# A DLRM tower on one core: the lookup of the last two tables goes behind the third lookup of the second step, and the Gram products of the first two tiles one lookup further down

## Chip, cores and metric

The kernel runs on one core of one Trainium2 chip. The metric is the device time of one execution in microseconds (us); the lower, the better. Engines are named as in the profile: PE (TensorE, matmuls), DVE (VectorE), ACT (ScalarE), POOL (GpSimd), SP (SyncE, which here only issues DMAs).

## What is computed

For each of 2048 items, 26 embedding rows of 128 numbers are looked up, set beside the item's dense vector, and all pairs of the 27 vectors are multiplied. The 351 products and the dense vector go through three layers.

```python
e = jnp.stack([tbl_f[ids[:, f]] for f in range(26)], axis=1)
combined = jnp.concatenate([e, r_dense_x[:, None, :]], axis=1)
z = jnp.einsum('bfd,bgd->bfg', combined, combined)[:, triu_i, triu_j]
h = jnp.concatenate([z.reshape(B, -1), r_dense_x], axis=1)
h = jnp.maximum(h @ W_top1 + b_top1, 0.0)      # 479 -> 512
h = jnp.maximum(h @ W_top2 + b_top2, 0.0)      # 512 -> 256
y = h @ W_top3                                 # 256 -> 1
```

## The kernel before

The 2048 items are cut into 16 tiles of 128; two tiles are a step, so there are 8 steps, counted from 0, and step 0 holds tiles 0 and 1. Each engine runs a program written out by hand, in order, and waits on semaphores.

The ten tables of 1000 rows are not gathered but multiplied by one-hot matrices on PE. Two such tables are a **unit**: `unit(t, o)` looks up tables 2o and 2o+1 for step t with 32 matmuls, in 8 fills of 4. Each fill needs one one-hot matrix, made by DVE (L620, six of the eight in steps 0 to 2) or ACT (L426 and L432, the other two); there are 12 one-hot buffers. `keep_unit` on ACT (L438) copies a unit's result out of PSUM. A table must first be loaded into `stage` and split into a high part (ACT, `chunk`, L417) and a low part (DVE, `chunk`, L610). The tables come in one after the other, table pair 4 (chunks 8 and 9) last. In the first two steps the units of both steps are mixed so that few tables are needed early; `FIRST_ORDER` sets that order, and with it the numbering of the one-hot fills on all engines.

The other 16 tables are gathered by POOL, one indirect DMA for each table and tile (L285, 256 in all). Four tables of one tile are a **quad**; the rows go through a ring of 8 buffers, and `quad(tile, k)` on PE (L768) transposes them.

`products(tile)` on PE (L783) makes the **Gram** products of one tile, in four banks of 16 matmul pairs that alternate between two PSUM buffers. It needs all five units of the tile's step. DVE (L638) copies banks 0 and 2, and ACT (L453) banks 1 and 3, into the one buffer `gram`. From the second tile on these copies first wait until the tile before has left `gram`. SP sends `gram` to DRAM (`spread`, 8 DMAs, L333, landing counted by `turn_out`) and fetches it back in another layout (`fetch_z`, 7 DMAs, L342). Layer 1 of step 0 on PE (L807, L809) stands behind the fourth quad of tile 2 and waits for `z` of both tiles 0 and 1:

```python
                if bank == 0:
                    for u in range(2):
                        pe.wait_ge(z_in[u], Z_DMAS * 16 * (t + 1))
```

SP's queue is in order as well. `load_ids(t, o)` (L311) brings the ids from which the one-hots of a unit are made; it waits until the ids that lay in that place have been used. Between the fetch of tile 0 and the spread of tile 1, SP issues the three loads of the layers' weights (`load_weights`, L321 to L323) and two loads of ids.

Of the kernel before, what the change touches and what calls it, by code (L numbers as in the profile page):

```python
# [29 lines left out]
FILLS = KT  # L30
BUFS = 12
ACT_STEPS, ACT_FILLS = 3, 2
DVE_FILLS = FILLS - ACT_FILLS
# [12 lines left out]
PIECES = ((0, OH_P // 16 * 16), (OH_P // 16 * 16, OH_P))  # L46
RING = 8

FIRST_ORDER = ((0, 0), (1, 0), (0, 1), (0, 2), (1, 1), (0, 3), (0, 4), (1, 2), (1, 3), (1, 4))

FIRST_PLACES = (2, 3, 4, 5, 0, 1, 2, 3, 4, 5)

# [46 lines left out]
def tower_kernel(nc, x, ids_g, ids_oh, gathered, oh_tables, w1_pairs, w1_dense, w2, w3, b1, b2, out):  # L99
    ctx = ExitStack()  # L100
    with ctx:
# [106 lines left out]
        def last_made(t):  # L208

            return (DVE_FILLS if t < ACT_STEPS else FILLS) - 1  # L210
# [87 lines left out]
        def _(sp):  # L298
# [5 lines left out]
            def load_ids(t, o):  # L304
                before = ids_before(t, o)
                if before:
                    sp.wait_ge(onehot_made, made_by_dve(*before, last_made(before[0])))
                    if act_makes(before[0], FILLS - 1):
                        sp.wait_ge(onehot_act, made_by_act(*before, FILLS - 1))
                i = ids_at(t, o)  # L310
                sp.dma_start(ids_b[:, i], ids_oh[t, o].partition_broadcast(P)).then_inc(ids_in[i], 16)  # L311
# [13 lines left out]
            def spread(tile):  # L325
                u = tile % 2
                for h in range(2):
                    sp.wait_ge(gram_kept[h], GBANKS // 2 * (tile + 1))
                if tile >= 2:
                    sp.wait_ge(z_in[u], Z_DMAS * 16 * (tile // 2))  # L330
                for s in range(S4 // 2 if tile == TILES - 1 else S4):
                    for src, to in strip_out(u, s):
                        sp.dma_start(to, src).then_inc(turn_out[u], 16)  # L333
# [41 lines left out]
                sp.dma_start(dst[:], src).then_inc(small_in, 16)  # L375
            load_x(1)
            load_ids(2, 0)
            spread(0)

            load_ids(2, 1)  # L380
            load_ids(2, 2)
            sp.wait_ge(chunk_l, NOH)
            fetch_z(0)
            load_weights()
# [28 lines left out]
        def _(act):  # L413
# [20 lines left out]
            def keep_unit(t, o):  # L434
                n = unit_at(t, o)
                act.wait_ge(onehot_used, fill_at(t, o, FILLS - 1) + 1)
                a = NV + UNIT * o
                nc.scalar.copy(by_vector(t % 2, a, a + UNIT, 0, STEP), ps_o[n % 2][:].rearrange("p f b -> p b f")).then_inc(unit_kept, 1)  # L438
# [9 lines left out]
            def keep_gram(tile):  # L448
                if tile:
                    act.wait_ge(turn_out[(tile - 1) % 2], TURN_DMAS * 16 * ((tile + 1) // 2))  # L450
                for h in range(1, GBANKS, 2):
                    act.wait_ge(gram_done, GBANKS * tile + h + 1)
                    nc.scalar.copy(gram_of(h), products_of(h)).then_inc(gram_kept[h % 2], 1)  # L453
# [68 lines left out]
            keep_unit(1, 1)  # L522
            keep_quad(1, 0)
            chunk(8)
            make(0, 4)
            keep_unit(0, 3)
            keep_quad(1, 1)
            chunk(9)
            make(1, 2)
            keep_unit(0, 4)  # L530
            keep_quad(1, 2)
            make(1, 3)
            keep_unit(1, 2)
            keep_gram(0)
            keep_quad(1, 3)
            make(1, 4)
            keep_unit(1, 3)
            keep_gram(1)
            make(2, 0)
            keep_unit(1, 4)  # L540
            act.wait_ge(small_in, 48)
            for t in range(1, STEPS - 1):
                a, b = 2 * t, 2 * t + 1
# [61 lines left out]
        @block.vector  # L605
        def _(dve):
            def chunk(n):
                dve.wait_ge(chunk_h, n + 1)
                at, (hi, lo) = parts_of(n)
                nc.vector.tensor_tensor(lo, at, f32(hi), ALU.subtract).then_inc(chunk_l, 1)  # L610

            def make(t, o, h):
                n = fill_at(t, o, h)
                if act_makes(t, h):
                    return
                if h == 0:
                    dve.wait_ge(ids_in[ids_at(t, o)], ids_loaded(t, o))
                if n >= BUFS:
                    dve.wait_ge(onehot_used, n - BUFS + 1)
                nc.vector.tensor_scalar(onehot[n % BUFS][0:OH_P, 0:FILL].rearrange("p (a b) -> p a b", a=RUNS),  # L620
                                        ids_b[0:OH_P, ids_at(t, o), :, 0:RUN], row_of[0:OH_P, h:h + 1], None, ALU.is_equal
                                        ).then_inc(onehot_made, 1)

            def makes(t, first, end):
                if t < STEPS:
                    for n in range(first, end):
                        make(t, n // FILLS, n % FILLS)

            def makes_of(n, first, end):

                t, o = FIRST_ORDER[n]
                makes(t, FILLS * o + first, FILLS * o + end)

            def keep_bank(tile, h):
                if tile and h == 0:
                    dve.wait_ge(turn_out[(tile - 1) % 2], TURN_DMAS * 16 * ((tile + 1) // 2))
                dve.wait_ge(gram_done, GBANKS * tile + h + 1)
                nc.vector.tensor_copy(gram_of(h), products_of(h)).then_inc(gram_kept[h % 2], 1)  # L638

            def keep_gram(tile):  # L640
                for h in range(0, GBANKS, 2):
                    keep_bank(tile, h)

            def keep_y(t):
                dve.wait_ge(w3_done, t + 1)
                if t:
                    dve.wait_ge(y_out, 32 * t)
                for u in range(2):
                    last = by_item(u)
                last.then_inc(y_made, 1)  # L650

            def by_item(u):
                p = HALF_P * u
                return nc.vector.tensor_copy(y_sb[p:p + 1, :].rearrange("p (g s) -> p s g", s=S4),  # L654
                                             ps_l[1][p:p + 1, 0, 0:TILE].rearrange("p (s g) -> p s g", s=S4))

            def keep_tail(u):
                dve.wait_ge(w3_done, STEPS + u)
                if u == 0:
                    dve.wait_ge(y_out, 32 * (STEPS - 1))  # L660
                by_item(u).then_inc(y_made, 1)

            dve.wait_ge(consts_made, 2)
            nc.vector.tensor_copy(row_of[:], row_i[:]).then_inc(row_made, 1)
            for i in range(2):
                nc.vector.memset(ps_g[i][:], 0.0).then_inc(gram_zeroed, 1)
            dve.wait_ge(row_made, 1)
            ALL = UNITS * FILLS
            makes_of(0, 0, DVE_FILLS)
            chunk(0)  # L670
            makes_of(1, 0, 2)
            chunk(1)
            makes_of(1, 2, 4)
            chunk(2)
            makes_of(1, 4, DVE_FILLS)
            chunk(3)
            makes_of(2, 0, DVE_FILLS)
            chunk(4)
            makes_of(3, 0, 3)
            chunk(5)  # L680
            makes_of(3, 3, DVE_FILLS)
            makes_of(4, 0, DVE_FILLS)
            chunk(6)
            makes_of(5, 0, 3)
            chunk(7)
            makes_of(5, 3, DVE_FILLS)
            chunk(8)
            makes_of(6, 0, 3)
            chunk(9)
            makes_of(6, 3, DVE_FILLS)  # L690
            makes_of(7, 0, DVE_FILLS)
            makes_of(8, 0, 2)
            keep_bank(0, 0)
            makes_of(8, 2, 4)
            keep_bank(0, 2)
            makes_of(8, 4, DVE_FILLS)
            makes_of(9, 0, 4)
            keep_bank(1, 0)
            makes_of(9, 4, DVE_FILLS)
            keep_bank(1, 2)  # L700
            makes(2, 0, BUFS)
            for t in range(1, STEPS - 1):
                a, b = 2 * t, 2 * t + 1
                makes(t + 1, BUFS, 4 * FILLS)
                keep_gram(a)
                makes(t + 1, 4 * FILLS, ALL)
                makes(t + 2, 0, FILLS)
                if t < STEPS - 2:
                    keep_y(t - 1)
                    keep_gram(b)  # L710
                    makes(t + 2, FILLS, BUFS)
                else:
                    keep_gram(b)
                    keep_y(t - 1)
            t, a, b = STEPS - 1, TILES - 2, TILES - 1
            keep_gram(a)
            keep_gram(b)
            keep_y(t - 1)
            keep_tail(0)
            keep_tail(1)  # L720

        @block.tensor
        def _(pe):
# [173 lines left out]
            quad(1, 0)  # L897
            unit(0, 3)
            quad(1, 1)
            unit(0, 4)  # L900
            quad(1, 2)
            unit(1, 2)
            products(0)
            quad(1, 3)
            unit(1, 3)
            products(1)
            unit(1, 4)
            pe.wait_ge(small_in, 48)
            for t in range(1, STEPS - 1):
                a, b = 2 * t, 2 * t + 1  # L910
# [101 lines left out]
```

## Time and profile before

| | us |
|---|---|
| median of 3 runs | 361.75 (360.04 to 362.33) |
| the profiled execution, its own time | 362.72 |
| its span, first to last instruction | 360.9 |
| PE busy | 335.2 (93%) |
| POOL busy | 247.5 (69%) |
| DVE busy | 229.0 (63%) |
| ACT busy | 155.2 (43%) |

The profile is one execution. Starts are in microseconds from the span's start. A timeline row merges like instructions that follow each other; the brackets at its end give the idle time before it and what ended that. The granted clock is a share of 2.4 GHz: 1.00 is 2.4 GHz, 0.50 is 1.2 GHz.

### The profile page before, as it was taken

The numbers are of one execution on the slowest core, as the hardware profiler recorded it, in microseconds if no ns is written. First come the engines' busy times: TensorE is split into PE (matmuls) and PEld (weight loads), VectorE is DVE, ScalarE is ACT, GpSimd is POOL, SyncE is SP. The second block draws the span as 40 slices with busy tenths as digits, with TensorE's granted clock in tenths as the row PEclk, the third lists the DMA queues.
The fourth block names the chain that finished last, engine by engine and source line by source line (L and its number), as shares of the span: only waits on it lengthen the run. The fifth ranks groups of instructions, "written<-read, shape, count | busy, mean of one in ns | idle before, by whom it ended". The sixth has DMA issues, their size and how long they took to land.

```text
span 360.9 us, 9694 instructions
## 1 busy us (share of the span) xinstructions
PE 335.2 (93%) x4080; PEld 315.3 (87%) x4080; DVE 229.0 (63%) x351; ACT 155.2 (43%) x271; POOL 247.5 (69%) x263
## 2 busy tenths in 40 slices
PE   0878889899999999999999999999999999889996
PEld 0768789899899989999899999999899999778885
DVE  5999794695267957689277957689286956101010
ACT  5779936487363223332333223332233323342432
POOL 4777777777777777777777777777777777773000
PEclk9989969999999999999999999999999999999999
DMA  7999212584243433434143433434143413343020
GB/s 187 251 245 238 60 53 61 155 270 141 56 138 95 126 87 104 121 108 117 53 123 102 129 95 102 119 111 117 53 128 96 125 53 101 90 123 97 14 70 5
DMA packets 31474, 40.76 MB, mean 113 GB/s; under 512 B 16864, under 2 KB 23984, under 8 KB 31431
## 3 DMA queue, kind: packets, MB, share of 16 engines
q1 hardware_dynamic: 22835, 22.97, 23.8%
q0 software_dynamic: 8192, 16.79, 16.7%
q8 instruction: 32, 0.52, 0.5%
q10 hardware_dynamic: 403, 0.38, 0.4%
q14 instruction: 12, 0.09, 0.1%
HBM read 32.75 MB, written 7.36 MB: 111 GB/s over the span
## 4 chain that ended last, share of the span: by engine, by line
PE 81%; DMA 6%; POOL 5%; ACT 4%; issue 3%; SPq 1%; ACTq 0%; DVE 0%
PE ps_o L738 36%; PE ps_g L783 15%; PE ps_l L807 10%; PE ps_t L768 7%; PE ps_l L833 7%; POOL rows L285 5%; PE ps_l L809 3%; DMA rows<-tbl,idx 2%; DMA turn<-gram 2%; ACT emb L445 1%; DMA idx<-ids_g 1%; PE ps_l L872 1%; ACT onehot L426 1%; SPq L333 1%; ACT emb L438 1%
## 5 line engine op out<-in xcount | busy, mean ns | idle before, releaser
L285 POOL DMA_INDIRECT rows<-tbl,idx x256 | 246.7, 964 | 80.6 <-issue 76.2
L620 DVE TENSOR_SCALAR onehot<-ids_b,row_of 125x513 fp32r<-125x513 int16 x290 | 192.6, 740 | 13.6 <-PE ps_o L738 7.8
L738 PE MATMUL ps_o<-onehot,tab 125*128 125x256 f32 x1248 | 161.0, 288 | 3.4 <-issue 3.4
L738 PEld LDWEIGHTS ps_o<-onehot,tab 125*128 125x128 f32 x1248 | 154.0, 193 | 3.7 <-issue 3.6
L638 DVE COPY gram<-ps_g 128x432 f32<-128x432 f32 x32 | 19.4, 607 | 87.8 <-PE ps_g L783 81.0
L438 ACT COPY emb<-ps_o 128x512 f32<-128x512 f32 x40 | 32.0, 799 | 77.3 <-PE ps_o L738 77.3
L783 PEld LDWEIGHTS ps_g<-emb 128*54 128x54 f32 x2048 | 53.8, 130 | 9.8 <-ACT emb L445 3.2
L783 PE MATMUL ps_g<-emb 128*54 128x54 f32 x2048 | 57.6, 214 | 4.0 <-ACT emb L445 2.5
L768 PE MATMUL ps_t<-ident,rows 128*128 128x128 f32 x256 | 38.5, 279 | 5.9 <-DMA rows<-tbl,idx 5.6
L445 ACT COPY emb<-ps_t 128x512 f32<-128x512 f32 (+1 forms) x65 | 42.3, 672 | 2.2 <-PE ps_t L768 1.8
L807 PE MATMUL ps_l<-z,w_sb 117*128 117x256 f32 x168 | 41.0, 379 | 0.2 <-issue 0.2
L768 PEld LDWEIGHTS ps_t<-ident,rows 128*128 128x128 f32 x256 | 29.3, 141 | 8.9 <-DMA rows<-tbl,idx 4.7
L807 PEld LDWEIGHTS ps_l<-z,w_sb 117*128 117x128 f32 x168 | 31.2, 189 | 4.5 <-issue 0.3
L453 ACT COPY gram<-ps_g 128x432 f32<-128x432 f32 x32 | 16.6, 520 | 42.3 <-PE ps_g L783 38.7
L459 ACT ACTIVATE h<-ps_l,b_sb 128x256 f32<-128x256 f32 x28 | 11.8, 471 | 37.3 <-PE ps_l L809 37.3
L426 ACT ACTIVATE onehot<-ids_b,row_act 125x513 fp32r<-125x513 int16 x30 | 20.2, 721 | 12.5 <-PE ps_o L738 9.6
L833 PE MATMUL ps_l<-h,w_sb 128*128 128x256 f32 x112 | 25.3, 379 | 0.0
L833 PEld LDWEIGHTS ps_l<-h,w_sb 128*128 128x128 f32 x112 | 20.7, 190 | 2.5
L654 DVE COPY y_sb<-ps_l 1x128 f32<-1x128 f32 x16 | 6.2, 389 | 23.5 <-PE ps_l L872 21.0
L432 ACT ACTIVATE onehot<-onehot 125x513 fp32r<-125x513 f32 x30 | 17.1, 620 | 0.0
L809 PE MATMUL ps_l<-xs,w_sb 128*128 128x256 f32 x56 | 16.7, 379 | 0.0
L610 DVE TENSOR_TENSOR tab<-stage,tab 125x1024 fp32r<-125x1024 f32 x10 | 12.3, 1228 | 4.2 <-ACT tab L417 4.2
(37 smaller groups left out, 82.6 us busy)
## 6 DMA issues: line engine op xcount, KB each, us to landing
turn<-gram SPq DMA_DIRECT2D x62, 91.1 KB
ids_b<-ids_oh SPq DMA_DIRECT2D x39, 129.0 KB, 3.6
stage<-tbl SPq DMA_DIRECT2D x10, 448.0 KB
rows<-tbl,idx POOLq DMA_INDIRECT x256
z<-turn SPq DMA_DIRECT2D x64, 40.5 KB
turn<-gram SPq DMA_DIRECT2D x62, 21.1 KB
xs<-x SPq DMA_DIRECT2D x8, 128.0 KB, 2.2
z<-turn SPq DMA_DIRECT2D x45, 4.5 KB
```

Source lines behind the costliest of these rows:

```text
L285: nc.gpsimd.indirect_dma_start(out=rows[m % RING][:, i, :], out_offset=None, in_=gathered[GATHERED.index(f)], in_offset=bass.IndirectOffse ...
L426: nc.scalar.activation(onehot[n % BUFS][0:OH_P, 0:FILL].rearrange("p (a b) -> p a b", a=RUNS), ids_b[0:OH_P, ids_at(t, o), :, 0:RUN], ACT. ...
L438: nc.scalar.copy(by_vector(t % 2, a, a + UNIT, 0, STEP), ps_o[n % 2][:].rearrange("p f b -> p b f")).then_inc(unit_kept, 1)
L445: nc.scalar.copy(by_vector(tile // 2 % 2, a, b, cols, cols + TILE), ps_t[m % 2][:, 0:b - a, :].rearrange("p f b -> p b f")).then_inc(quad_ ...
L620: nc.vector.tensor_scalar(onehot[n % BUFS][0:OH_P, 0:FILL].rearrange("p (a b) -> p a b", a=RUNS), ids_b[0:OH_P, ids_at(t, o), :, 0:RUN], r ...
L638: nc.vector.tensor_copy(gram_of(h), products_of(h)).then_inc(gram_kept[h % 2], 1)
L738: last = nc.tensor.matmul(ps_o[n % 2][:, j, :], tab[0:OH_P, UNIT * o + j, part, h, :], onehot[m % BUFS][0:OH_P, STEP * j:STEP * (j + 1)], ...
L768: last = nc.tensor.transpose(ps_t[m % 2][:, i, :], rows[m % RING][:, i, :], ident[:])
L783: last = nc.tensor.matmul(ps_g[h % 2][HALF_P * q:HALF_P * q + GCOLS, GCOLS * g:GCOLS * (g + 1)], v, v, start=True, stop=True)
L807: nc.tensor.matmul(ps_l[bank][:, i, :], w1_part(2 * bank + i, blk), z_part(t, blk, 0, 2), start=blk == 0, stop=False)
L809: last = nc.tensor.matmul(ps_l[bank][:, i, :], w1_part(2 * bank + i, DB), xs[t % 2][:], start=False, stop=True)
L833: last = nc.tensor.matmul(ps_l[0][:, n, :], w2_sb[:, c, P * n:P * (n + 1)], h1[:, c, :], start=(c, n) == (0, 0), stop=(c, n) == (N1 - 1, N ...
```

## The change

`FIRST_ORDER` gets `(1, 2)` ahead of `(0, 4)`, so that the unit of tables 8 and 9 for step 0 comes one unit later, on PE, ACT and DVE alike. On PE `products(0)` now stands behind `unit(1, 3)`, the ninth unit, and `products(1)` behind `unit(1, 4)`, the tenth. The copies of the Gram banks on DVE and ACT move with them. DVE makes three more one-hot fills ahead of `chunk(8)`. On SP the ids of `(2, 1)` and `(2, 2)` are loaded ahead of `spread(0)` and no longer behind it. No work is added or removed.

```diff
-FIRST_ORDER = ((0, 0), (1, 0), (0, 1), (0, 2), (1, 1), (0, 3), (0, 4), (1, 2), (1, 3), (1, 4))
+FIRST_ORDER = ((0, 0), (1, 0), (0, 1), (0, 2), (1, 1), (0, 3), (1, 2), (0, 4), (1, 3), (1, 4))
@@ SP
             load_x(1)
             load_ids(2, 0)
-            spread(0)
-
             load_ids(2, 1)
             load_ids(2, 2)
+            spread(0)
+
             sp.wait_ge(chunk_l, NOH)
             fetch_z(0)
             load_weights()
@@ ACT
             chunk(8)
-            make(0, 4)
+            make(1, 2)
             keep_unit(0, 3)
             keep_quad(1, 1)
             chunk(9)
-            make(1, 2)
-            keep_unit(0, 4)
+            make(0, 4)
+            keep_unit(1, 2)
             keep_quad(1, 2)
             make(1, 3)
-            keep_unit(1, 2)
-            keep_gram(0)
+            keep_unit(0, 4)
             keep_quad(1, 3)
             make(1, 4)
             keep_unit(1, 3)
-            keep_gram(1)
+            keep_gram(0)
             make(2, 0)
             keep_unit(1, 4)
+            keep_gram(1)
@@ DVE
             makes_of(5, 3, DVE_FILLS)
+            makes_of(6, 0, 3)
             chunk(8)
-            makes_of(6, 0, 3)
+            makes_of(6, 3, DVE_FILLS)
             chunk(9)
-            makes_of(6, 3, DVE_FILLS)
             makes_of(7, 0, DVE_FILLS)
-            makes_of(8, 0, 2)
+            makes_of(8, 0, DVE_FILLS)
+            makes_of(9, 0, 4)
             keep_bank(0, 0)
...
@@ PE
             quad(1, 1)
+            unit(1, 2)
+            quad(1, 2)
             unit(0, 4)
-            quad(1, 2)
-            unit(1, 2)
-            products(0)
             quad(1, 3)
             unit(1, 3)
+            products(0)
+            unit(1, 4)
             products(1)
-            unit(1, 4)
             pe.wait_ge(small_in, 48)
```

On PE, from the quad (1, 2) to the first quad of tile 2, a unit is a row of 32 matmuls on `ps_o`, a quad a row of 4 on `ps_t`, and the products of a tile a row of 64 pairs on `ps_g`:

```order
 L768 MATMUL ps_t<-ident,rows 128x128 x4
 L738 MATMUL ps_o<-onehot,tab 128x256 x32
-L783 MATMUL ps_g<-emb 54x54 x64
 L768 MATMUL ps_t<-ident,rows 128x128 x4
 L738 MATMUL ps_o<-onehot,tab 128x256 x32
 L783 MATMUL ps_g<-emb 54x54 x64
 L738 MATMUL ps_o<-onehot,tab 128x256 x32
+L783 MATMUL ps_g<-emb 54x54 x64
 L768 MATMUL ps_t<-ident,rows 128x128 x4
```

Each tile's products went one unit down, those of tile 1 to the place right ahead of tile 2's first quad.

On DVE, from the chunk 7 to the last copy of tile 1's Gram; L610 is the low part of a table, L620 a one-hot fill, L638 a copy of a Gram bank:

```order
-L620 TENSOR_SCALAR onehot<-ids_b,row_of 125x513 x3
+L620 TENSOR_SCALAR onehot<-ids_b,row_of 125x513 x6
 L610 TENSOR_TENSOR tab<-stage,tab 125x1024
 L620 TENSOR_SCALAR onehot<-ids_b,row_of 125x513 x3
 L610 TENSOR_TENSOR tab<-stage,tab 125x1024
-L620 TENSOR_SCALAR onehot<-ids_b,row_of 125x513 x11
+L620 TENSOR_SCALAR onehot<-ids_b,row_of 125x513 x16
 L638 COPY gram<-ps_g 128x54x8
 L620 TENSOR_SCALAR onehot<-ids_b,row_of 125x513 x2
 L638 COPY gram<-ps_g 128x54x8
```

Three fills moved ahead of chunk 8, and the first Gram copy now has sixteen fills ahead of it since chunk 9, in place of eleven.

## Rows read from the trace of the kernel before

**Rows 1.** The page: TensorE's busy time; granted clock in 40 slices.
```profile
PE 335.2 (93%) x4080; PEld 315.3 (87%) x4080; DVE 229.0 (63%) x351; ACT 155.2 (43%) x271; POOL 247.5 (69%) x263
...
PEclk9989969999999999999999999999999999999999
```

**Rows 2.** PE timeline, 0 to 62: start, us busy, work [idle before, releaser].
```profile
22.94 1.11 PE L768 MATMUL ps_t<-ident,rows 128*128 128x128 f32 x4 [2.54 <-DMA rows<-tbl,idx]
23.70 4.95 PE L738 MATMUL ps_o<-onehot,tab 125*128 125x256 f32 x32
...
42.91 0.60 PE L768 MATMUL ps_t<-ident,rows 128*128 128x128 f32 x4
46.87 6.82 PE L738 MATMUL ps_o<-onehot,tab 125*128 125x256 f32 x32 [3.36 <-issue]
...
57.84 3.53 PE L783 MATMUL ps_g<-emb 128*54 128x54 f32 x128
```

**Rows 3.** Stretches: busy time by engine, granted clock, DMA share, GB/s.
```profile
47.00:50.00 3.00, 3.00 (x15) 3.00 (x16) 3.00 (x6) 0.14 (x1) 2.39 (x3) 0.50 0.18 49
50.00:53.10 3.10, 3.10 (x16) 3.10 (x16) 3.10 (x6) 2.36 (x4) 2.19 (x4) 0.50 0.14 42
```

**Rows 4.** DVE timeline, 36 to 64.
```profile
41.17 1.23 DVE L610 TENSOR_TENSOR tab<-stage,tab 125x1024 fp32r<-125x1024 f32 x1 [1.25 <-ACT tab L417]
...
45.54 1.23 DVE L610 TENSOR_TENSOR tab<-stage,tab 125x1024 fp32r<-125x1024 f32 x1 [1.17 <-ACT tab L417]
46.68 7.29 DVE L620 TENSOR_SCALAR onehot<-ids_b,row_of 125x513 fp32r<-125x513 int16 x11
```

**Rows 5.** ACT timeline, 36 to 64.
```profile
44.43 1.08 ACT L417 CAST tab<-stage 125x1024 fp32r<-125x1024 f32 x1
```

**Rows 6.** PE timeline, 60 to 96.
```profile
68.93 1.81 PE L783 MATMUL ps_g<-emb 128*54 128x54 f32 x64 [1.43 <-DVE gram L638]
70.67 4.04 PE L738 MATMUL ps_o<-onehot,tab 125*128 125x256 f32 x32
74.54 0.60 PE L768 MATMUL ps_t<-ident,rows 128*128 128x128 f32 x4
...
87.67 1.53 PE L807 MATMUL ps_l<-z,w_sb 117*128 117x256 f32 x6
```

**Rows 7.** SP's DMA queue, 60 to 90: start, us issuing, work.
```profile
62.01 2.93 SPq L333 DMA_DIRECT2D turn<-gram  x8
65.04 0.83 SPq L311 DMA_DIRECT2D ids_b<-ids_oh  x2
68.30 2.56 SPq L342 DMA_DIRECT2D z<-turn  x7
...
72.21 1.15 SPq L311 DMA_DIRECT2D ids_b<-ids_oh  x2
73.45 4.17 SPq L333 DMA_DIRECT2D turn<-gram  x8
83.32 2.54 SPq L342 DMA_DIRECT2D z<-turn  x7
```

**Rows 8.** SP's DMA queue, 95 to 250.
```profile
98.98 2.84 SPq L333 DMA_DIRECT2D turn<-gram  x8
103.92 2.53 SPq L342 DMA_DIRECT2D z<-turn  x7
...
197.48 3.09 SPq L333 DMA_DIRECT2D turn<-gram  x8
203.09 2.53 SPq L342 DMA_DIRECT2D z<-turn  x7
```

**Rows 9.** Chain of waits, 345 to 356: start, us, what.
```profile
350.89 1.77 DMA z<-turn
```

**Rows 10.** The gather line: nanoseconds min/median/max, first and last start.
```profile
L285 POOL DMA_INDIRECT rows<-tbl,idx x256: 940/945/2087, 4.4 to 327.9; - x128
```

**Rows 11.** PE timeline, 320 to 361.
```profile
340.06 0.65 PE L768 MATMUL ps_t<-ident,rows 128*128 128x128 f32 x4
```

More of the change, by code:

```diff
@@ L686, in _ @@
             makes_of(5, 3, DVE_FILLS)
+            makes_of(6, 0, 3)
             chunk(8)
-            makes_of(6, 0, 3)
+            makes_of(6, 3, DVE_FILLS)
             chunk(9)
-            makes_of(6, 3, DVE_FILLS)
             makes_of(7, 0, DVE_FILLS)
-            makes_of(8, 0, 2)
+            makes_of(8, 0, DVE_FILLS)
+            makes_of(9, 0, 4)
             keep_bank(0, 0)
-            makes_of(8, 2, 4)
+            makes_of(9, 4, DVE_FILLS)
             keep_bank(0, 2)
-            makes_of(8, 4, DVE_FILLS)
-            makes_of(9, 0, 4)
+            makes(2, 0, 4)
             keep_bank(1, 0)
-            makes_of(9, 4, DVE_FILLS)
+            makes(2, 4, FILLS)
             keep_bank(1, 2)
-            makes(2, 0, BUFS)
+            makes(2, FILLS, BUFS)
             for t in range(1, STEPS - 1):
```

## Prediction

> **What bounds the kernel now.** I read the page first. PE is busy for 335.2 of 360.9 us, and its granted clock is full except in two early places, in the third slice and, more strongly, in the sixth [rows 1]. So the end is set by PE's own queue, and what can be won is idle PE time and time at the lower clock. Next come PE's timeline and the stretches around the sixth slice. PE stands idle for 3.36 us ahead of the unit of tables 8 and 9, which starts at 46.87, and that unit then takes 6.82 us, where one at full clock takes 4.04 [rows 2, 6]. The granted clock is 0.50 (1.2 GHz) over that unit [rows 3]. The timeline of DVE says what ended the wait: the low part of table 9 starts at 45.54 and takes 1.23 us, to 46.77, 0.1 us ahead of the unit. It had itself waited for ACT's high part, which ended at 44.43 + 1.08 = 45.51 [rows 4, 5].
>
> The third view is SP's queue, since the change moves the place at which the Gram leaves. From the spread of tile 0 a chain runs to PE's layer 1. The spread starts at 62.01, the fetch of tile 0 at 68.30, then the weights, ids at 72.21, the spread of tile 1 at 73.45 and the fetch of tile 1 at 83.32 [rows 7]. The seven DMAs of that fetch are issued by 83.32 + 2.54 = 85.86. The profile has no row for their landing, but at the tail the same kind of fetch lands 1.77 us after its last issue [rows 9], so I estimate 85.86 + 1.77 = 87.6. Layer 1 starts at 87.67, with no idle time ahead of it [rows 6]. **The z of tile 1 has therefore no slack at all**: PE is not waiting for it, but would if it came there any earlier.
>
> **The early wait goes.** The unit that now stands at 43.3 uses tables 4 and 5, which are long split. Its first three fills are made ahead of chunk 8, in some 3 x 0.66 = 2.0 us, of which 1.25 is DVE's wait for ACT there. Chunk 8 thus starts 0.7 us late, the other three fills end near 45.1, and DVE's wait of 1.17 us ahead of chunk 9 takes the 0.7 up [rows 4]. Those fills are the fourth to sixth, due on PE from 44.8 on. So the wait of 3.36 and the slow clock's 6.82 - 4.04 = 2.78 go: 6.1 us.
>
> **What takes some of it back on the way.** The unit of tables 8 and 9 starts at about 42.91 + 0.38 + 3.87 + 0.38 = 47.5. Here 3.87 is a unit (70.67 to 74.54), and 0.38 a quad: from 74.54 to 87.67 stand three units and four quads, and (13.13 - 3 x 3.87) / 4 = 0.38 [rows 2, 6]. Its table is ready at 46.8, but DVE makes its six fills only from 46.68 on, at 7.29 / 11 = 0.66 each [rows 4]; the sixth is there at 50.7, three eighths of the unit (1.45) follow, and it ends at 52.1 and not at 51.4. That costs 0.7. ACT's two fills for it no longer wait for a late PE, so they hide. The products of tile 0 now have three units and three quads between 42.91 and their start: 42.91 + 3 x 0.38 + 3 x 3.87 + 0.7 = 56.4, in place of 57.84 [rows 2]. The unit that is added there eats most of the 6.1 us won.
>
> DVE's sixteen fills up to the first Gram copy end at 46.68 + 16 x 0.66 = 57.2, and the first bank is ready about a microsecond into the products, so those hide. Rows for the quads (1, 2) and (1, 3), wanted 6 to 9 us sooner, are the other thing needed early; POOL's gathers run without regard to PE, and I price them at nothing here, with a rival below.
>
> **The chain over SP.** The spread of tile 0 starts 62.01 - 57.84 = 4.17 after the products [rows 2, 7], so at 60.5. From a spread's start to its fetch took 6.29 here, with two loads of ids issued at 65.04 in between, which the change puts ahead of the spread [rows 7]. Later, with nothing in between, it took 4.94 and 5.61 [rows 8]; I take the middle, 5.28. The fetch of tile 0, which also frees the copies of tile 1's Gram, then starts at 60.5 + 5.3 = 65.8 and not at 68.30: 2.5 us sooner. All that SP does after it stands as before: weights, ids, spread of tile 1 (5.15 us behind the fetch of tile 0), fetch of tile 1 (9.87 behind that spread, about twice the usual 5.28), landing. Of these I expect the same 19.4 us from 68.30 to 87.67. The products of tile 1 are done well ahead of their spread's place in the queue, as before: their second half starts 0.63 us behind the fetch of tile 0 and takes 1.81, so ends near 68.3, and SP comes to them at 65.8 + 5.15 = 71.0 [rows 6, 7].
>
> So layer 1 can start at 65.8 + 19.4 = 85.2: 2.5 us sooner than before. **PE comes there much earlier.** The unit (1, 4) no longer stands behind the products of tile 1, so PE goes from their second half to tile 2's quad in 70.67 - 68.93 = 1.74, and from there to layer 1 in 13.13: 65.8 + 0.63 + 1.74 + 13.13 = 81.3. It then waits 3.9 us for z, a wait that the profile of before doesn't have. Queued behind it on PE are layer 1 itself, the products of tile 2 and all the rest, and nothing there can go ahead.
>
> **What the wait does to the clock.** Two early waits show the price. After 2.54 us idle a quad and a unit took 1.11 + 4.95, where later ones take 0.60 + 4.04: 1.42 more. After 3.36 us idle it was 2.78 [rows 2, 6]. The new wait is nearer to the second and longer, so I take 2.8, with 1.4 below and, if every microsecond from 47 to 53.1 ran at half speed, 6.1 / 2 = 3.1 above [rows 3]. The Trainium skill, "TensorE: Matmul & The Clock Gate", section "HAM oscillation — how this bites in real kernels", counts the penalty as half of the time spent at the lower clock. By it the same stretch would have cost that 3.1 and not 2.78, and the sum would be 0.3 us worse; the measured row stands here.
>
> **The sum.** Layer 1 starts 2.5 us sooner and loses 2.8 us to the clock: +0.3 us. From layer 1 on PE has hardly a wait up to the tail, and nothing of the change lies there. POOL doesn't hold the end either, before or after: its last gather starts at 327.9 and PE takes the last quad at 340.06 [rows 10, 11]. The profiled execution took 362.72 (span 360.9 and 1.8 around it), so 363.0 by it. It is 0.97 above the median of the runs, and I carry that difference over: 361.75 + 0.3 = 362.05. A measurement of this kernel, whose runs lie 2.3 us apart, tells about 1% (3.6 us) from no change, and this is far inside.
>
> **Rivals.** (a) *The ids were not what slowed the turn of tile 0.* The Trainium skill, "DMA: Bandwidth & Descriptors", section "Queues, rings and completion order", says that an engine takes up the descriptors of one ring in order; by that, loads issued behind the spread could not delay it much. As a mechanism of this kernel: the 6.29 us stays, the fetch of tile 0 starts at 60.5 + 6.3 = 66.8, the gain at layer 1 is 1.5, the wait there and its clock cost stay, and it comes out 1.3 us slower: 363.1. It decides the sign from 4.9 us on, since 68.30 - 60.5 - 2.8 is that. For it: one later turn took 5.61 with no ids behind it, not so far from 6.29. Against it: the other took 4.94, and the ids are the only thing that tells this turn from the later ones.
>
> (b) *The clock hardly falls* or falls as after the 2.54 us wait: 2.5 sooner and 0 to 1.4 lost, so 359.3 to 360.7. For it: two waits only, with prices a factor of two apart. Against it: both waits cost something, and the new one is the longest of the three.
>
> (c) *z comes as early as PE does.* Then layer 1 starts at 81.3, 6.4 us sooner, with no clock lost: 355.4. For that, the 9.87 us of tile 1's turn would have to shrink by 3.9. Only less traffic could do it, but the weights ahead of it are the same bytes in the same queue.
>
> (d) *The rows of quads (1, 2) and (1, 3) are late.* A wait of 2 us there would push the products of tile 0 and the whole chain by as much, with 1.4 us of clock beside it if it is long: up to 3.4 slower at layer 1, 365.5. The stretches there show the DMA share at 0.18 and 0.14 [rows 3], so I expect them in time.
>
> **How the numbers follow.** The forecast as reckoned 0.45, (a) 0.27, (b) 0.15, (c) 0.08, (d) 0.05. The bounds: turn of 4.94 and a clock cost of 1.4 give -1.4 us, with no cost at all -2.8 (358.9); a turn of 6.29 with 3.1 gives +1.6 (363.4). With the 0.6 us by which the highest run stood above the median this reaches 364.0; I take 358.6 to 364.0, which leaves out (c), (d) and little else. Faster by over 1% needs (c) or something near it: 0.11. Slower by over 1% needs (d) and more: 0.06. Within 1%: 0.83.
>
> **What the new profile would show.** Right: no idle time of PE near 43 to 47 and full clock there; the products of tile 0 from about 56.4; a fetch of tile 0 near 65.8; tile 2's first quad near 68.2, where it was at 74.54; then an idle PE of 3.9 us ahead of L807, put down to the DMA of z, ending near 85.2, and a granted clock of 0.50 behind it. Wrong: layer 1 with no wait ahead of it (then it is (c), and the time near 355), a wait of PE for rows before 55 (d), or a first spread-to-fetch of 6.3 us (a). What would upset all of it is a slower turn of tile 1 than 9.87, since the weights and ids there now meet other gathers, or a wait that appears past layer 1.

## The result, and the profile after

Over 20 runs the changed kernel took 362.58 us (361.18 to 364.64). The kernel before, now with 20 runs as well, took 360.89 us (358.6 to 363.7). The ratio of the runs is 1.0049, with a 95% interval of 1.0031 to 1.0067: 0.3 to 0.7% slower, some 1.7 us, inside the 1% forecast as no change. Ratios, here and below, leave out disturbed runs, that is, those over 1.5% above the fastest of their kernel. The profiled execution of the changed kernel took 361.37 us, which is 1.35 less than the profiled one of before (362.72) and 1.2 below its own median. The two traces show the mechanism, but not the size of the difference between the medians.

The page of the changed kernel, lines as in [rows 1]:

```profile
span 359.6 us, 9694 instructions
...
PE 335.4 (93%) x4080; PEld 314.7 (88%) x4080; DVE 228.8 (64%) x351; ACT 154.7 (43%) x271; POOL 247.1 (69%) x263
...
PEclk9989999998999999999999999999999999999999
```

The lower clock of the sixth slice is gone; the tenth, from 81 to 90 us, now has an 8. PE's busy time is the same. PE's timeline of the changed kernel, answering to [rows 2, 6]:

```profile
42.81 0.60 PE L768 MATMUL ps_t<-ident,rows 128*128 128x128 f32 x4
43.17 4.04 PE L738 MATMUL ps_o<-onehot,tab 125*128 125x256 f32 x32
47.04 0.60 PE L768 MATMUL ps_t<-ident,rows 128*128 128x128 f32 x4
47.53 4.88 PE L738 MATMUL ps_o<-onehot,tab 125*128 125x256 f32 x32
...
56.56 3.53 PE L783 MATMUL ps_g<-emb 128*54 128x54 f32 x128
...
68.23 0.66 PE L768 MATMUL ps_t<-ident,rows 128*128 128x128 f32 x4
...
80.94 0.60 PE L768 MATMUL ps_t<-ident,rows 128*128 128x128 f32 x4
84.98 2.37 PE L807 MATMUL ps_l<-z,w_sb 117*128 117x256 f32 x6 [3.44 <-issue]
...
93.75 3.60 PE L783 MATMUL ps_g<-emb 128*54 128x54 f32 x128
97.28 0.66 PE L768 MATMUL ps_t<-ident,rows 128*128 128x128 f32 x4
```

The last two of these rows in the kernel before:

```profile
94.75 3.60 PE L783 MATMUL ps_g<-emb 128*54 128x54 f32 x128
98.28 0.66 PE L768 MATMUL ps_t<-ident,rows 128*128 128x128 f32 x4
```

Read it from above. The 3.36 us of idle time ahead of the second unit are gone, and the unit of tables 4 and 5 takes 4.04 us. The unit of tables 8 and 9 starts at 47.53 and lasts 4.88. The products of tile 0 start at 56.56 and tile 2's first quad at 68.23, where it was at 74.54. So far PE is 6.3 us ahead. Then comes a row that the trace of before doesn't have: 3.44 us of idle time ahead of L807 at 84.98, and behind it the first six matmuls of layer 1 take 2.37 us in place of 1.53. Layer 1 starts 2.69 us sooner than before and ends, at 93.75, only 1.00 us sooner than before, at 94.75. It took 94.75 - 87.67 = 7.08 us before and takes 8.77 now.

SP's DMA queue of the changed kernel, answering to [rows 7]:

```profile
60.73 2.84 SPq L333 DMA_DIRECT2D turn<-gram  x8
65.87 2.55 SPq L342 DMA_DIRECT2D z<-turn  x7
...
71.36 3.47 SPq L333 DMA_DIRECT2D turn<-gram  x8
80.76 2.54 SPq L342 DMA_DIRECT2D z<-turn  x7
```

The fetch of tile 0 starts at 65.87, 5.14 us behind the spread; the spread of tile 1 at 71.36; and from there to its fetch pass 9.40 us. Its last DMA is issued by 80.76 + 2.54 = 83.30, and with the 1.77 us of [rows 9] z lands near 85.1. Layer 1 starts at 84.98, which points to z as what PE waits for. The profile itself calls this wait "issue", that is, names no releaser, where the prediction had it put down to the DMA of z; the experiments below, which take the weights from ahead of tile 1's turn, bear z out.

The stretches of the changed kernel, with the granted clock as the third number from the end:

```profile
46.00:50.00 4.00, 4.00 (x31) 3.54 (x29) 4.00 (x7) 3.36 (x7) 3.09 (x4) 1.00 0.42 83
...
85.60:88.90 3.30, 3.30 (x10) 2.59 (x9) 0.00 (x0) 0.00 (x0) 2.56 (x3) 0.50 0.52 162
89.00:93.00 4.00, 4.00 (x20) 3.50 (x19) 0.00 (x0) 0.84 (x2) 3.01 (x4) 1.00 0.18 50
```

The clock is 1.00 over the unit of tables 8 and 9, 0.50 (1.2 GHz) right behind the new wait, and 1.00 again from 89 on. DVE's timeline of the changed kernel, answering to [rows 4]:

```profile
41.73 1.22 DVE L610 TENSOR_TENSOR tab<-stage,tab 125x1024 fp32r<-125x1024 f32 x1
...
45.50 1.23 DVE L610 TENSOR_TENSOR tab<-stage,tab 125x1024 fp32r<-125x1024 f32 x1 [0.59 <-ACT tab L417]
46.64 10.56 DVE L620 TENSOR_SCALAR onehot<-ids_b,row_of 125x513 fp32r<-125x513 int16 x16
57.62 0.61 DVE L638 COPY gram<-ps_g 128x432 f32<-128x432 f32 x1 [0.41 <-PE ps_g L783]
```

Chunk 8 starts 0.56 us later, DVE's wait ahead of chunk 9 takes that up, and the sixteen fills are done 0.4 us ahead of the first Gram bank.

### The profile page after: what moved, and what is told of

Its sections match the earlier page's. It is cut to its first block, busy times and chain, and to the rows that moved or that the text cites. A ratio compares the mean times of both kernels' runs of the same rounds, so it can differ in the third digit from the quotient of the medians.

```text
span 359.6 us, 9694 instructions
## 1 busy us (share of the span) xinstructions
PE 335.4 (93%) x4080; PEld 314.7 (88%) x4080; DVE 228.8 (64%) x351; ACT 154.7 (43%) x271; POOL 247.1 (69%) x263
## 4 chain that ended last, share of the span: by engine, by line
PE 83%; DMA 5%; POOL 5%; issue 3%; ACT 2%; SPq 1%; ACTq 0%; DVE 0%
PE ps_o L738 37%; PE ps_g L783 15%; PE ps_l L807 11%; PE ps_t L768 8%; PE ps_l L833 7%; POOL rows L285 5%; PE ps_l L809 3%; DMA rows<-tbl,idx 2%; DMA turn<-gram 1%; DMA idx<-ids_g 1%; PE ps_l L872 1%; ACT emb L445 1%; SPq L333 1%; PE ps_g L856 1%; DMA z<-turn 1%
## 5 line engine op out<-in xcount | busy, mean ns | idle before, releaser
L620 DVE TENSOR_SCALAR onehot<-ids_b,row_of 125x513 fp32r<-125x513 int16 x290 | 192.6, 741 | 15.3 <-PE ps_o L738 11.0
L738 PE MATMUL ps_o<-onehot,tab 125*128 125x256 f32 x1248 | 159.6, 286 | 0.0
L738 PEld LDWEIGHTS ps_o<-onehot,tab 125*128 125x128 f32 x1248 | 152.0, 190 | 0.8
L638 DVE COPY gram<-ps_g 128x432 f32<-128x432 f32 x32 | 19.4, 607 | 87.3 <-PE ps_g L783 77.1
L807 PE MATMUL ps_l<-z,w_sb 117*128 117x256 f32 x168 | 42.3, 389 | 3.4 <-issue 3.4
L807 PEld LDWEIGHTS ps_l<-z,w_sb 117*128 117x128 f32 x168 | 32.1, 194 | 8.3 <-issue 3.6
L755 PE MATMUL ps_o<-onehot,tab 125*128 125x256 f32 x32 | 6.1, 375 | 9.2 <-DVE onehot L620 9.2
```

Of the source, the lines that this page charges most:

```text
L738: last = nc.tensor.matmul(ps_o[n % 2][:, j, :], tab[0:OH_P, UNIT * o + j, part, h, :], onehot[m % BUFS][0:OH_P, STEP * j:STEP * (j + 1)], ...
L807: nc.tensor.matmul(ps_l[bank][:, i, :], w1_part(2 * bank + i, blk), z_part(t, blk, 0, 2), start=blk == 0, stop=False)
```

## The experiments

Twelve runs were made, of seven kernels, some of them repeated. They fell into six sessions, each with the kernel before beside them. In four of these, with ten of the runs, every median lay between 495 and 504 us, that of the kernel before too; only two of the twelve ran where the kernel before took 361. I call the four the long sessions. The traces of the long sessions have a PE that gets its matmuls singly over long stretches. These rows are from the changed kernel there, inside one unit:

```profile
44.64 0.37 PE L738 MATMUL ps_o<-onehot,tab 125*128 125x256 f32 x1 [1.73 <-issue]
48.14 0.37 PE L738 MATMUL ps_o<-onehot,tab 125*128 125x256 f32 x1 [3.13 <-issue]
```

Single matmuls of 0.37 us stand behind 1.73 and 3.13 us of idle time, and no releaser is named. Since PE waits there for something else, I draw nothing on a difference of 1% from the times of such sessions. What stands between two DMAs, or whether PE waits ahead of layer 1, can still be read from their traces.

### The products of tile 2 ahead of layer 1 (label products_first)

```diff
                 quad(a, 3)
+                if t == 1:
+                    products(a)
                 layer1(t - 1, 0)
                 layer1(t - 1, 1)
-                products(a)
+                if t > 1:
+                    products(a)
```

The same was done with `keep_gram(a)` on ACT. What was expected:

> The changed kernel with one step moved on PE, ACT and DVE: in the first round of the loop the Gram products of tile 2 and their copies stand ahead of layer 1 of step 0, where PE otherwise waits for the z of tile 1. Theory (PE comes to layer 1 3.4 us ahead of z and pays for it twice, idle and at the lower clock): 3.5 us of products fill the wait, layer 1 starts near 85 with no idle time and at full clock, and the kernel is 3.4 + 1.7 = 5.1 us faster than the changed one and 3.4 us faster than before. Rival 1 (the price is in the landing of z alone): layer 1 starts at 85 but the clock falls all the same, 3.4 us faster than the changed one. Rival 2 (the copies of tile 2's Gram wait for tile 1's turn, so the products wait too): within 1 us of the changed kernel.

Measured: 357.48 us against 361.19 for the kernel before in that session, a ratio of 0.9912 (0.9886 to 0.9937). That is 3.2 us faster than before, and with the 1.0049 of the changed kernel, (1.0049 - 0.9912) x 361 = 4.9 us faster than the changed one, measured in another session; with both intervals that is 3.8 to 6.1 us, an estimate. The theory said 5.1, rival 1 said 3.4, rival 2 within 1. The granted clocks of the timed runs go with the theory: 12 of the 13 runs have 0.995 or 1.00, where of the changed kernel's 20 runs 7 have 0.995 and the others less. It is also faster than both kernels of this study. PE's timeline in its trace:

```profile
80.58 0.60 PE L771 MATMUL ps_t<-ident,rows 128*128 128x128 f32 x4
84.10 4.80 PE L786 MATMUL ps_g<-emb 128*54 128x54 f32 x128 [2.92 <-ACT emb L445]
88.83 1.56 PE L810 MATMUL ps_l<-z,w_sb 117*128 117x256 f32 x6
...
95.85 0.60 PE L771 MATMUL ps_t<-ident,rows 128*128 128x128 f32 x4
```

Layer 1 (here L810) follows at 88.83 with no wait, and tile 3's first quad starts at 95.85, where it was at 97.28 in the changed kernel and at 98.28 before. But the wait had not gone in this execution, it had another releaser: 2.92 us ahead of the products, which then took 4.80 instead of 3.60. ACT's timeline says why:

```profile
80.51 1.34 ACT L426 ACTIVATE onehot<-ids_b,row_act 125x513 fp32r<-125x513 int16 x2 [2.65 <-DMA ids_b<-ids_oh]
```

ACT waited 2.65 us for ids of step 2, and the copy of the last quad, which the products need, stood behind that. The path of the theory held, with layer 1 free of a wait, but what took its place was another wait and another stretch at the lower clock. This execution, at 361.62 us the second longest of the 13 of its kernel, shows less than the median won; that the usual run loses less there is inferred from the times alone. SP's queue of the same trace gives the changed kernel's chain a second sample, since up to the fetch of tile 1 the two kernels have the same queue:

```profile
65.50 2.54 SPq L342 DMA_DIRECT2D z<-turn  x7
...
72.36 3.23 SPq L333 DMA_DIRECT2D turn<-gram  x8
83.26 2.54 SPq L342 DMA_DIRECT2D z<-turn  x7
```

The turn of tile 1 took 10.90 us here, 1.5 more than in the changed kernel's trace. By the same estimate as above z lands at 83.26 + 2.54 + 1.77 = 87.6, which is when layer 1 started before the change.

### The weights ahead of the spread of tile 0 (label weights_early_4)

```diff
             load_ids(2, 2)
-            spread(0)
-
             sp.wait_ge(chunk_l, NOH)
-            fetch_z(0)
             load_weights()
             load_ids(2, 3)
             load_ids(2, 4)
+            spread(0)
+            fetch_z(0)
```

> The changed kernel with the layers' weights and the ids of (2, 3) and (2, 4) loaded ahead of the spread of tile 0, as soon as the tables are split; once more, for a session in which the kernel before takes 361 us. Theory (z of tile 1 holds layer 1, because its turn stands behind the weights in SP's queue): the spread of tile 1 starts once its Gram is kept, near 69, is through in some 5.2 us, z lands near 79, PE reaches layer 1 at 81.2 with no wait and full clock, ACT no longer waits for the ids of (2, 3) as it did for 2.65 us with the products of tile 2 put first, and the kernel is 5 us faster than the changed one and 3.5 us faster than before. Rival (the wait ahead of layer 1 is on something else, or the gain is given back at a later wait): the time stays within 1 us of the changed kernel.

Measured: 360.39 us against 360.76, a ratio of 0.9995 (0.9959 to 1.0031), so the time of before and some 2 us less than the changed kernel. That is neither the 5 us of the theory nor the rival's "within 1 us of the changed kernel". SP's queue:

```profile
65.25 2.88 SPq L333 DMA_DIRECT2D turn<-gram  x8
70.41 2.54 SPq L342 DMA_DIRECT2D z<-turn  x7
73.53 3.62 SPq L333 DMA_DIRECT2D turn<-gram  x8
79.74 2.54 SPq L342 DMA_DIRECT2D z<-turn  x7
```

With neither the weights nor the two loads of ids right ahead of it the turn of tile 1 took 6.21 us, against 9.40 in the changed kernel. z's fetch is issued by 82.28, and with 1.77 more it is there at 84.1. PE's timeline (L767 is a quad, L806 layer 1):

```profile
55.17 0.83 PE L767 MATMUL ps_t<-ident,rows 128*128 128x128 f32 x4 [2.98 <-DMA rows<-tbl,idx]
55.66 5.49 PE L737 MATMUL ps_o<-onehot,tab 125*128 125x256 f32 x32
61.08 3.53 PE L782 MATMUL ps_g<-emb 128*54 128x54 f32 x128
...
85.54 0.60 PE L767 MATMUL ps_t<-ident,rows 128*128 128x128 f32 x4
85.97 1.46 PE L806 MATMUL ps_l<-z,w_sb 117*128 117x256 f32 x6
...
92.99 3.62 PE L782 MATMUL ps_g<-emb 128*54 128x54 f32 x128
```

Layer 1 starts at 85.97, right behind the quad at 85.54, with no wait: that part of the theory held. But the quad at 55.17, (1, 3), waited 2.98 us for gathered rows, and the unit behind it took 5.49 us at a lower clock. SP issued the weights from 46.5 and the two loads of ids from 50.5, and the DMA share from 48 to 54 was 0.82 to 1.01, where the changed kernel has 0.12 to 0.25. POOL started the last gather of this quad at 48.87, 1.0 us later than in the changed kernel, and its rows were there 6.3 us behind that start, where in the changed kernel it was 4.4 at most (from 47.85 to the quad at 52.25). The products of tile 0 start at 61.08, 4.5 us later than in the changed kernel, and that is what was given back. The forecast for rows named this wait as its rival (d); here the early loads brought it about.

The same kernel had run in three long sessions. Label weights_early:

> The changed kernel with the layers' weights and the ids of (2, 3) and (2, 4) loaded ahead of the spread of tile 0, as soon as the tables are split. Theory (z of tile 1 holds layer 1, because its turn stands behind the weights in SP's queue): the spread of tile 1 starts once its Gram is kept, near 69, is through in some 5.2 us, z lands near 79, PE reaches layer 1 at 81.3 with no wait and full clock, and the kernel is 5 us faster than the changed one and 3.5 us faster than before. Rival (the wait ahead of layer 1 is on something else, or the gain is given back at a later wait): the time stays within 1 us of the changed kernel.

501.75 us, a ratio of 0.9968 (0.9932 to 1.0003). Label weights_early_2:

> The changed kernel with the layers' weights and the ids of (2, 3) and (2, 4) loaded ahead of the spread of tile 0, as soon as the tables are split; once more, since in the first session every kernel took over 490 us. Theory (z of tile 1 holds layer 1, because its turn stands behind the weights in SP's queue): the spread of tile 1 starts once its Gram is kept, near 69, is through in some 5.2 us, z lands near 79, PE reaches layer 1 at 81.2 with no wait and full clock, and the kernel is 5 us faster than the changed one and 3.5 us faster than before. Rival (the wait ahead of layer 1 is on something else, or the gain is given back at a later wait): the time stays within 1 us of the changed kernel.

499.57 us, 0.994 (0.9897 to 0.9984). Label weights_early_3, with six runs:

> The changed kernel with the layers' weights and the ids of (2, 3) and (2, 4) loaded ahead of the spread of tile 0, as soon as the tables are split; a third time, since in its first two sessions every kernel took over 490 us. Theory (z of tile 1 holds layer 1, because its turn stands behind the weights in SP's queue): the spread of tile 1 starts once its Gram is kept, near 69, is through in some 5.2 us, z lands near 79, PE reaches layer 1 at 81.2 with no wait and full clock, and the kernel is 5 us faster than the changed one and 3.5 us faster than before. Rival (the wait ahead of layer 1 is on something else, or the gain is given back at a later wait): the time stays within 1 us of the changed kernel.

495.88 us, 0.9874 (0.9805 to 0.9943). None of the three times decides between theory and rival. The traces say more than the times. In all three, and in the next kernel's, layer 1 follows its quad with no wait and its first six matmuls take 1.46 us. In the four traces of long sessions that have PE's new order and the weights ahead of tile 1's turn (after_again, after_again_2, ids_back, ids_back_2) PE stands idle for 2.2 to 2.9 us there. So the wait ahead of layer 1 hangs on what stands ahead of that turn.

### The weights at 55 us (label weights_mid)

```diff
             load_ids(2, 2)
+            load_ids(2, 3)
+            load_ids(2, 4)
+            sp.wait_ge(chunk_l, NOH)
+            load_weights()
             spread(0)
-
-            sp.wait_ge(chunk_l, NOH)
             fetch_z(0)
-            load_weights()
-            load_ids(2, 3)
-            load_ids(2, 4)
```

> The changed kernel with the ids of (2, 3) and (2, 4) and then the layers' weights loaded ahead of the spread of tile 0, so that the weights go out near 55 us, 8.5 us later than where they delayed the rows of quad (1, 3). Theory (z of tile 1 is late because its turn stands behind the weights, and what the early weights won went to the late rows): PE waits neither for rows at 52 nor ahead of layer 1, the turn of tile 0 may take up to 1.5 us more behind the end of the weights, layer 1 starts near 81 to 83, and the kernel is 3 to 5 us faster than the changed one, that is 1.5 to 3.5 us faster than before. Rival (the same bytes cost the same wherever they stand, since gathers or turns meet them everywhere): 360.5, the time with the weights at 46.5.

It met a long session: 495.98 us against 496.7, a ratio of 0.9988 (0.9952 to 1.0024). Whether it wins its 3 to 5 us is open. PE has no wait ahead of layer 1 in its trace. Its DMA queue shows the turn of tile 1 all the same, first this kernel's, then that of the changed kernel in another long session (label after_again_2):

```profile
109.35 3.57 SPq L333 DMA_DIRECT2D turn<-gram  x8
115.22 2.53 SPq L342 DMA_DIRECT2D z<-turn  x7
```

```profile
100.31 2.84 SPq L333 DMA_DIRECT2D turn<-gram  x8
104.72 2.54 SPq L342 DMA_DIRECT2D z<-turn  x7
...
110.59 3.30 SPq L333 DMA_DIRECT2D turn<-gram  x8
120.35 2.55 SPq L342 DMA_DIRECT2D z<-turn  x7
```

From the spread of tile 1 to its fetch: 5.87 us without the weights ahead of it, 9.76 with them. Over all fourteen traces of the study it took 8.4 to 10.9 us in the nine where the weights and the two loads of ids stand right ahead, and 5.2 to 6.3 in the five where they don't. This step is shown, in both kinds of session; how much of it is the weights' and how much the ids' was not tried.

### The ids of step 2 behind the spread again (labels ids_back, ids_back_2)

```diff
+            spread(0)
+
             load_ids(2, 1)
             load_ids(2, 2)
-            spread(0)
-
```

> The changed kernel with the ids of (2, 1) and (2, 2) loaded behind the spread of tile 0 again, as before. Theory: the turn of tile 0 takes 6.3 us in place of 5.1, the z of tile 1 and layer 1 come about 1.1 us later, PE comes to them later too, so its wait stays near 3.4 us, and the kernel is about 1.1 us slower than the changed one (some 2.8 us slower than before). Rival: the turn takes 5.1 us with the ids behind it too, and the time is that of the changed kernel.

500.77 us (0.992, 0.9871 to 0.9969). Once more:

> The changed kernel with the ids of (2, 1) and (2, 2) loaded behind the spread of tile 0 again, as before; once more, since in its first session every kernel took over 490 us. Theory (the ids lengthened the turn of tile 0): the turn of tile 0 takes 6.3 us in place of 5.1, the z of tile 1 and layer 1 come about 1.1 us later, PE comes to them later too, so its wait stays near 3.4 us, and the kernel is about 1.1 us slower than the changed one. Rival (a ring's descriptors are taken up in order, so what is issued behind the turn doesn't slow it): the turn takes 5.1 us with the ids behind it too, and the time is that of the changed kernel.

495.93 us (0.9945, 0.9901 to 0.999). Both met long sessions. SP's queue of the second:

```profile
100.64 2.86 SPq L333 DMA_DIRECT2D turn<-gram  x8
103.60 0.83 SPq L311 DMA_DIRECT2D ids_b<-ids_oh  x2
105.03 2.57 SPq L342 DMA_DIRECT2D z<-turn  x7
```

The turn of tile 0 took 4.39 us with the ids issued right behind it, and 4.41 without, in the same session (104.72 - 100.31 above); the other session with both gave 4.43 and 4.40. So there the ids cost it nothing, which is what the rival said. At 361 us it took 6.29 with them (one trace, the kernel before) and 5.14 to 5.19 without (three traces). Two other traces of long sessions, without the ids behind, had 5.14 and 5.39, so the turn varies by a microsecond for other reasons too. Whether the 1.1 us is the ids' doing is left open.

### The same part alone in the kernel before (label ids_first)

The diff is that of the change, on SP only.

> The kernel before with one part of the change alone: on SP the ids of (2, 1) and (2, 2) are loaded ahead of the spread of tile 0. Theory (the chain over SP sets layer 1, and the ids lengthened the turn of tile 0): the turn goes from 6.3 to about 5.1 us, PE's wait of 1.43 us in the products of tile 1 shrinks to about 0.3, the z of tile 1 lands as much sooner, and the kernel is 1.1 us faster than before. Rival (an engine takes up a ring's descriptors in order, so loads issued behind the turn don't slow it): the turn stays at 6.3 us and the time at that of before.

502.01 us, a ratio of 0.9959 (0.9912 to 1.0006), in a long session: undecided.

### PE kept busy in the wait (label pe_kept_busy)

```diff
                 if bank == 0:
+                    if t == 0:
+                        for i in range(36):
+                            nc.tensor.transpose(ps_l[0][:, 0, 0:TILE], ident[:], ident[:])
                     for u in range(2):
```

> The changed kernel with 36 extra transposes of the identity matrix (some 3.4 us at full clock) ahead of PE's wait for z in layer 1 of step 0, into a PSUM buffer that layer 1 then overwrites; the results don't depend on them. They take away no wait, only PE's idleness in it. Theory (the wait costs twice, as idle time and through the clock behind it): layer 1 starts near 85.0 as in the changed kernel, but at full clock, and the kernel is 1.7 us faster than the changed one, at the time of before. Rival (the clock doesn't depend on it, or the loss is elsewhere): the time of the changed kernel, and a granted clock of 0.50 behind 85 as there.

500.32 us, a ratio of 0.9916 (0.9859 to 0.9973), in a long session, so its time says nothing on 1.7 us. Its trace:

```profile
126.94 5.26 PE L799 MATMUL ps_l<-ident 128*128 128x128 f32 x31 [0.45 <-issue]
132.04 1.46 PE L810 MATMUL ps_l<-z,w_sb 117*128 117x256 f32 x6
```

The first six matmuls of layer 1 take 1.46 us, full clock, where those of the changed kernel, in the trace of its first long session, took 2.90 behind 2.51 us of idle time. But the transposes filled more than the wait. By SP's queue z's last DMA was issued at 121.43 + 2.60 = 124.03, so z was there near 125.8, and layer 1 began 6.2 us later; PE was starved up to 126.5, and it was the transposes that ran slowly, 31 of them in 5.26 us where 36 were expected to take 3.4. The trace thus doesn't show that keeping PE busy in the wait pays.

### The changed kernel again (labels after_again, after_again_2)

> The changed kernel as it is, for its granted clock and its wait ahead of layer 1 once more. Theory: 1.7 us slower than before, with an idle PE of 3.4 us ahead of layer 1 and one or two stretches at 0.50 behind it; if it is how long the clock stays low that tells its runs apart, a run with more of it is the slower one by about half of the extra time. Rival: the spread from run to run comes from the landing of z, and the wait ahead of layer 1 differs by as much.

502.91 us (0.9984, 0.9943 to 1.0026). Once more:

> The changed kernel as it is, for its granted clock and its wait ahead of layer 1 once more; again, since in its first session every kernel took over 490 us. Theory: 1.7 us slower than before, with an idle PE of 3.4 us ahead of layer 1 and one or two stretches at 0.50 behind it; if it is how long the clock stays low that tells its runs apart, a run with more of it is the slower one by about half of the extra time. Rival: the spread from run to run comes from the landing of z, and the wait ahead of layer 1 differs by as much.

495.7 us (0.9953, 0.9911 to 0.9996). Both met long sessions, and these ratios are below 1 where that of the session at 361 us is 1.0049. Nothing follows for the spread from run to run. The wait ahead of layer 1 is in both traces, 2.51 and 2.93 us, with the first six matmuls at 2.90 behind it.

## Why the prediction was right, and what was off

The path was foreseen: the early wait goes, and a new one comes ahead of layer 1, because z is late. The forecast of no change held; its 0.3 us did not, and that it had the right sign is in part luck, as the sum below shows.

**What bounds it, and the missing slack of z.** Right. Layer 1 could start with z and no sooner: 84.98, where 85.2 was forecast. In the five traces in which tile 1's turn is short, the wait ahead of layer 1 is gone.

**The early wait goes.** Right, with its clock: nothing idle between 43 and 47, and 4.04 us for the unit.

**What is taken back on the way.** The unit of tables 8 and 9 was to start at 47.5 and lose 0.7 us to DVE's fills. It started at 47.53 and took 4.88 us, 0.84 over 4.04. The products of tile 0 came at 56.56 (56.4).

**The chain over SP.** The spread of tile 0 came at 60.73 (60.5), its fetch at 65.87 (65.8), and the rest of the chain kept its length: 84.98 - 65.87 = 19.1 (19.4). PE stood ready at 81.5 (81.3). Rival (a) had the turn at 6.3, and it was 5.14. What the rival rests on, that ids behind a turn cost it nothing, was borne out by two pairs of traces from the long sessions all the same.

**The clock behind the new wait.** Mis-sized in the profiled execution: 2.8 was forecast, and layer 1 took 93.75 - 84.98 = 8.77 in place of 7.08, so 1.69. It lies between the two rows that I had, 1.42 and 2.78. I had taken the price from the length of the wait, and that is the step that failed here: behind 3.36 us of idle time the trace of before has the clock at 0.50 for all of 47.0 to 53.1 [rows 3], 6.1 us, and behind 3.44 us the changed one has it there for 3.3 us, 85.6 to 88.9. What sets how long it stays low was not found.

**The sum against the medians.** The direction was right, slower, and the size too small: 0.3 us forecast, 1.7 measured. The step that fell short is the last one, "It is 0.97 above the median of the runs, and I carry that difference over". With 20 runs the profiled execution of before lies 1.83 above the median, and that of the changed kernel 1.21 below. And the gap is wider than 1.4 us. With its terms as the two traces have them, 1.69 lost to the clock and 2.69 won at the start of layer 1, the sum is not +0.3 but -1.0 us, 2.7 from the medians. The clock cost, put 1.1 too high, hid a part of that: here two errors met by luck.

What made the profiled execution of before slow can be read in part. Its mean granted clock was 0.986. In the two sessions at 361 us only 5 of 26 undisturbed runs of the kernel before had that, 6 had 0.99 and 15 had 0.995 or more; the medians of the first two groups are 361.6 and 361.5 us, and the 13 runs at 0.995 have 360.5. An estimate: a mean of 0.986 is 2 x 0.014 x 361 = 10.1 us at 0.50, and the trace has two such stretches, of 3.4 us from 22.4 on and of 6.8 from 46.2 on. A mean of 0.995 is 3.6 us, which has room for a short one but not for the long one. So a usual run of before loses less than 2.78 us behind the early wait, and the win from removing it was put too high by one microsecond or more. No trace of a usual run of before was taken, so this is argued and not shown. Nor is it all: at equal clocks the changed kernel is slower too, 362.4 (7 runs) against 360.5 us at 0.995, and 362.7 (11 runs) against 361.5 at 0.99. The turn of tile 1, which took 9.40 us in one trace and 10.90 in another with the same queue, may hold the rest: with 10.90 the gain at layer 1 would be nothing, and its clock cost would stay. That too is argued, and the cause of the gap stays open.

**What the experiments settled.** That the gain of 6.3 us at tile 2's first quad was lost ahead of and in layer 1 is shown by the products moved into the wait: by the medians 4.9 us (3.8 to 6.1) came back of the 3.4 + 1.7 that the trace puts there. That the wait is long because tile 1's turn stands behind the weights and the ids is shown by the turn's 6.21 and 5.87 us without them, and by layer 1, which has no wait in any of the five such traces. How the loss in layer 1 divides between idle time and clock rests on the two traces, and on the higher granted clocks with the products moved, since the experiment for it met a starved PE.

## What to carry to other kernels

When a wait on the critical path goes, follow the engine to its next wait on something that has its own pace, and see how much slack that has now: here z had none, and 6.3 us of head start became 1.0. Put work of the same engine into the wait that is left, ahead of trying to hurry the transfer: here the first won 4.9 us and the second 2, against the changed kernel. Large loads moved to a quiet stretch of the DMA engines meet the small gathers there: look at who waits for rows in that stretch first. And before a sum of two microseconds is set against a median, ask of the profiled execution whether its granted clock is that of the usual run.

## What the runs showed that was not expected

- In the sessions of the experiments the kernel before took 361 us twice and 497 to 504 four times, with PE's matmuls coming singly and 0.3 to 3.1 us apart, no releaser named, and a mean granted clock of 0.87. What starves it was not found.
- The wait of PE for gathered rows, 2.98 us, with the three loads of weights (702, 256 and 512 KB by the trace) in a stretch where the DMA share before was 0.14 to 0.18 [rows 3].
- The turn of tile 0 took 4.3 to 4.4 us in eight of the ten traces of the long sessions, 5.1 and 5.4 in the two others, and 5.1 to 6.3 in the four traces at 361 us.
- In the session of weights_mid one run of that kernel took 861 us and one of the kernel before 864, both with a mean granted clock of 1.00. Nothing on record explains them.
